# A graph network's convolution: adding and folding two tables of sums with strided reductions in the loop

## The chip, the cores and the metric

The kernel runs on one core of a Trainium2 chip. The metric is the device time of one execution in microseconds, and the median over several executions is compared. The engines of the core are PE (matrix products), DVE (vector work), ACT (activations and copies), POOL (here it only issues gathers from DRAM by index) and SP (here it only issues plain transfers).

## The reference

12500 nodes with 256 features, 212500 edges sorted by their target `dst`, and two layers. The first is a convolution, the second an attention; a residual and a layer norm follow each. What is computed around the change is the end of the first layer:

```python
mids = jnp.concatenate([mid0, mid1, mid2.reshape(-1, 3 * MUL), mid3.reshape(-1, 3 * MUL)], axis=1)
agg = jax.ops.segment_sum(mids, edge_dst, num_segments=n)
agg = agg * (1.0 / math.sqrt(NUM_NEIGHBORS))
z0a = agg[:, :MUL]
z0b = agg[:, MUL:2 * MUL]
z1a = agg[:, 2 * MUL:5 * MUL].reshape(n, MUL, 3)
z1b = agg[:, 5 * MUL:].reshape(n, MUL, 3)
o0 = (z0a @ lin2_w00 + z0b @ lin2_w01) * a * inv2
o1 = (jnp.einsum('nuc,uv->nvc', z1a, lin2_w10) + jnp.einsum('nuc,uv->nvc', z1b, lin2_w11)) * a[:, :, None] * inv2
```

`MUL` is 64, and `mid1` is itself a sum over three components; the kernel stores these three apart and adds them up per node, not per edge.

## The kernel before

**Stages.** `project_sources` writes a table of projected node rows (`y`). `convolve_in_order` (tensors named `sub_...`) is the first layer, `attend_in_order` (`ord_...`) the second. They run one after the other.

**The convolution's loop.** Edges come in tiles of 128. A group has 12 tiles (six pairs, numbered `u` from 0 to 5; four runs of three tiles), a turn of the loop three groups (`b` is 0, 1 or 2). There are 139 groups, so 47 turns. For each tile POOL issues one gather of 128 rows of `y` into `xg` (line 993). For each pair DVE multiplies these rows with edge weights (`products`, lines 1328 and 1333) and makes two selection matrices (line 1313); PE sums the products by target node into `psum_a` (`add_up`, line 1044) and makes the weights of a later pair (line 1024). ACT copies each run's sums out, and SP adds them to DRAM. It doesn't accumulate there: runs go in turn to one of two tables, `sums[0]` and `sums[1]`, each run over the zeros that the one before it in the same table had put behind its own rows. A node's sum is therefore the sum of its rows in both tables.

**Order.** Each engine walks the same list of steps, written by hand, and they meet in semaphores. POOL waits, ahead of every second tile, until PE has summed all but the last 8 to 10 tiles in front of it (`agg_done` at 12 g + k - 8 for tile k of group g). DVE waits for the rows, for the weights and for its buffers.

**The node step.** From the second turn on, each turn but the last also finishes one pair of node tiles (2 x 128 nodes): 45 pairs in the loop (`LOOP_PAIRS`), four in a tail behind it (`TAIL_PAIRS`). SP loads the pair's rows of both tables, those of `sums[0]` to `node_rows[:, 0]` and those of `sums[1]` to `loop_odds`, each 2 x 5 x 128 numbers wide (640 a node: chunk 0, three chunks for the three components, chunk 4). In the middle group, behind the products of pair 1, DVE runs `fold` for tile 0 and tile 1 of the pair (lines 1340 to 1353, called from `with_products`). It adds the two tables (line 1344, once for both tiles), waits for its own result, and then for each tile sums the left halves of chunks 1 to 3 into 64 numbers (line 1351) and copies their right halves beside them (line 1352), into `fold_rows`. PE turns chunk 0, the two halves of `fold_rows` and chunk 4 over (`turn_sums`, line 1057), tile 0 behind pair 2 and tile 1 behind pair 3 of the same group. Later in the turn come the products with `lin2`, the residual, the layer norm (statistics at line 1376, scaling at 1392, in the next turn) and the projection for the attention. `fold`, `turn_sums` and the rest are called for the four tail pairs too, whose second tables lie in `loop_odds` or in parts of `xg`.

Lines that the steps below name beside these: 2326 is the attention's gather on POOL, 2657 its leaky slope (`ord_raw` with itself), 2759 its weighting (`ord_xg` by `ord_prob`, which lies in PSUM), 266 a maximum in the set-up, 1364 and 1366 the residual's multiply-adds (the latter with every third number).

Of the kernel before, what the change touches and what calls it, by code (L numbers as in the profile page):

```python
# [22 lines left out]
AX = mybir.AxisListType.X  # L23

P = 128
# [3 lines left out]
MUL = 64  # L29
# [33 lines left out]
LOOP_PAIRS = SUB_TURNS - 2  # L63
TAIL_PAIRS = NODE_PAIRS - LOOP_PAIRS
# [40 lines left out]
def is_pair(i, n):  # L105

    return type(i) is int and i == n
# [646 lines left out]
def convolve_in_order(nc, io, c, y, sums, x1, xpa, att, kept):  # L754
# [10 lines left out]
    with Phase(nc, "sub", kept) as ph:  # L765
# [11 lines left out]
        agg_s = ph.sb("agg_s", [P, SUB_TURN, GROUP_SUBS, 4 * MUL])  # L777
        start_b = c["sub_start_b"]
        zeros = ph.sb("zeros", [P, SUM_WIDE])
        node_rows = ph.sb("node_rows", [P, TAIL_PAIRS, 2, 5, P])  # L780
        loop_odds = ph.sb("loop_odds", [P, 2, 5, P])
        spare = [xg[:, 1, 0:5], xg[:, 1, 5:10], xg[:, 2, 0:5]]
        node_odds = [loop_odds[:]] + [r.rearrange("p k f -> p (k f)").rearrange("p (j q f) -> p j q f", j=2, q=5)
                                      for r in spare]
        node_xt = ph.sb("node_xt", [P, TAIL_PAIRS, 2, 2, P])
        node_x = ph.sb("node_x", [P, TAIL_PAIRS, 2, FEAT])
        fold_rows = ph.sb("fold_rows", [P, 2, 2 * P])
        rows_t = ph.sb("rows_t", [P, 2, 4, P])
        pre = ph.sb("pre", [P, 2, FEAT])
        stats = ph.sb("stats", [P, 2, 6])  # L790
# [7 lines left out]
        psum_h = ph.ps("h", [P, 512])  # L798
        psum_w = ph.ps("w", [P, 4, 512])
# [14 lines left out]
        sums_in = [ph.sem(f"sums_in{n}") for n in range(TAIL_PAIRS)]  # L814
# [3 lines left out]
        both_added = ph.sem("both_added")  # L818
        folded, turned, turned_copied = ph.sem("folded"), ph.sem("turned"), ph.sem("turned_copied")
# [33 lines left out]
        def pair_rows(table, n):  # L853
# [4 lines left out]
        tail = [(LOOP_PAIRS + e, (e + 1) % TAIL_PAIRS, LOOP_PAIRS + 1 if e == TAIL_PAIRS - 1 else 1, (e + 1) % 2,  # L858
                 e // 2 + 1 + (LOOP_PAIRS if e % 2 else 0)) for e in range(TAIL_PAIRS)]

        with nc.Block(no_gpsimd_drain=True) as block:
# [141 lines left out]
            def _(pe):  # L1003
# [45 lines left out]
                    elif j == RUN - 1:  # L1049
                        mm.then_inc(evens_summed, 1)  # L1050

                def turn_sums(n, j, buf, bank):

                    pe.wait_ge(folded, 2 * n + j + 1)
                    for q, of in enumerate((node_rows[:, buf, j, 0], fold_rows[:, j, 0:P], fold_rows[:, j, P:],
                                            node_rows[:, buf, j, 4])):
                        mm = nc.tensor.transpose(bank[:, q * P:(q + 1) * P], of, c["ident"][:])
                    mm.then_inc(turned, 1)

# [31 lines left out]
                def bank_of_hidden(i, b, u, g):  # L1091

                    if normed_pair(i) and b == 0:
                        if u == 2:
                            if has(i, b, 1):
                                pe.wait_ge(silu_done, 2 * g + 4)
                            else:
                                pe.wait_ge(pre_done, LOOP_PAIRS)
                            turn_normed(i - 2, 0, psum_h)
                        if u == 3:  # L1100
                            project(i - 2, 0, psum_h)
                        if u == 4:
                            pe.wait_ge(p_copied, 2 * i - 3)
                            project(i - 2, 1, psum_h)
                    if sums_pair(i) and b == 1:
                        if u == 2:
                            pe.wait_ge(silu_done, 2 * g + 4)
                            turn_sums(i - 1, 0, 0, psum_h)
                        if u == 3:
                            pe.wait_ge(turned_copied, 2 * i - 1)  # L1110
                            turn_sums(i - 1, 1, 0, psum_h)
                    if sums_pair(i) and (b, u) == (2, 2):
                        pe.wait_ge(silu_done, 2 * g + 4)
                        add_self(i - 1, 0, i, psum_h)
# [42 lines left out]
                for e in range(TAIL_PAIRS + 1):  # L1157
                    if e == 0:
                        for j in range(2):
                            turn_sums(tail[0][0], j, tail[0][1], psum_w[:, j])  # L1160
                    if e < TAIL_PAIRS:
                        n, buf, times, _, _ = tail[e]
                        if e > 1:
                            pe.wait_ge(pre_done, n - 1)
                        add_self(n, buf, times, psum_w[:, 2 + e % 2])
                    if e > 0:
                        n, _, _, buf, _ = tail[e - 1]
                        if e > 1:
                            pe.wait_ge(t_copied, n)
                        turn_normed(n, buf, psum_a[0])  # L1170
                        for j in range(2):
                            pe.wait_ge(p_copied, 2 * n + j - 1)
                            project(n, j, (psum_a[1], psum_h)[j])
                    if e + 1 < TAIL_PAIRS:
                        n, buf, _, _, _ = tail[e + 1]
                        for j in range(2):
                            pe.wait_ge(turned_copied, 2 * n + j - 1)
                            turn_sums(n, j, buf, psum_w[:, j])

            @block.scalar  # L1180
            def _(act):
# [98 lines left out]
            def _(dve):  # L1280
# [39 lines left out]
                def products(g, b, i, u):  # L1320
# [16 lines left out]
                            .to_broadcast(shape), ALU.mult)  # L1337
                    a.then_inc(mids_done, 2)

                def fold(n, j, buf, times, first):  # L1340

                    if j == 0:
                        dve.wait_ge(sums_in[buf], 32 * times)
                        nc.vector.tensor_tensor(node_rows[:, buf], node_rows[:, buf], node_odds[buf],
                                                ALU.add).then_inc(both_added, 1)
                    if not first:
                        dve.wait_ge(turned, 2 * n + j - 1)
                    if j == 0:
                        dve.wait_ge(both_added, n + 1)
                    f, rows = fold_rows[:, j], node_rows[:, buf, j]  # L1350
                    nc.vector.tensor_reduce(f[:, 0:MUL], rows[:, 1:4, 0:MUL].rearrange("p q f -> p f q"), AX, ALU.add)
                    nc.vector.tensor_copy(f[:, MUL:].rearrange("p (q f) -> p q f", f=MUL), rows[:, 1:4, MUL:])\
                        .then_inc(folded, 1)
# [42 lines left out]
                def with_products(i, b, u):  # L1396

                    if normed_pair(i) and (b, u) == (0, 1):
                        normalise(i - 2, 0, None if is_pair(i, 2) else i - 2, is_pair(i, 2))
                    if sums_pair(i) and (b, u) == (1, 1):  # L1400
                        fold(i - 1, 0, 0, i, is_pair(i, 1))
                        fold(i - 1, 1, 0, i, is_pair(i, 1))
                    if sums_pair(i) and (b, u) == (2, 4):
                        add_x(i - 1, 0, i, psum_h, is_pair(i, 1))
                    if sums_pair(i) and (b, u) == (2, 5):
                        moments(i - 1)
# [1738 lines left out]
```

## Time and profile before

| | |
|---|---|
| time, median of 3 runs | 4435.05 us (4433.04 to 4443.15) |
| the profiled execution, its time | 4443.72 us |
| its span | 4442.3 us |
| granted TensorE clock, mean | 0.916 |
| PE, weight loads, DVE, ACT, POOL busy | 89%, 56%, 82%, 28%, 73% of the span |
| convolution's gathers (line 993) | 1662, the first at 83.4 us, the last at 2218.9 us |
| attention's gathers (line 2326) | 1666, from 2294.3 to 4397.7 us |

A row of the trace names the line, the engine, the operation, what it writes and from what, the shapes (partitions x numbers) and the count. In a time line the first two numbers are start and duration in microseconds, and a bracket at the end is the idle time of the engine before it, with what ended it. "issue" in such a bracket is idle time in which the engine waited for nothing that the profile shows. In a view of one line, three durations in nanoseconds stand as minimum/median/maximum, then the first and the last start. In a group of the page, the first number behind the bar is busy time in microseconds, the second the mean duration in nanoseconds, and behind the second bar stands the idle time ahead.

### The profile page before, as it was taken

What the parts mean: (1) busy time and instruction counts of PE and PEld (TensorE: products, weight loads), DVE (VectorE), ACT (ScalarE), POOL (GpSimd) and SP (SyncE); (2) the same over time, 40 slices, a digit from 0 to 9 for tenths busy, and PEclk for the clock granted to TensorE, in tenths of its full rate; (3) what the DMA queues carried; (4) which work ended last, traced back from release to release, by engine and by line L of the source; (5) the groups of instructions that cost most, each with busy time, mean ns of one, the idle gap of its engine ahead of it and who ended that gap; (6) DMA issues with size and microseconds to landing.
All of it is one profiled execution on the core that took longest, in us unless ns stands there. A gap on an engine that the chain in (4) does not pass through costs nothing. (4 is left out here: it accounts for less than half of the span.)

```text
span 4442.3 us, 107936 instructions
## 1 busy us (share of the span) xinstructions
PE 3946.7 (89%) x29492; PEld 2493.8 (56%) x29492; DVE 3633.5 (82%) x10373; ACT 1263.3 (28%) x3082; POOL 3245.2 (73%) x3375
## 2 busy tenths in 40 slices
PE   6899999999999999899958899889999888998997
PEld 5444444444444444444436666666667666666665
DVE  2788888888888888888838888888888888888887
ACT  4222222222222222222212222222232222222222
POOL 3777777777777777777727777777777777777774
PEclk8999999999999999999968888888888889888888
DMA  7666666666666667666644444444444444444443
GB/s 284 189 203 205 194 208 200 201 205 194 209 199 200 207 194 210 198 201 205 193 136 122 123 124 125 123 123 124 124 123 124 124 123 123 124 124 123 123 125 84
DMA packets 443567, 727.04 MB, mean 164 GB/s; under 512 B 147552, under 2 KB 279666, under 8 KB 443492
## 3 DMA queue, kind: packets, MB, share of 16 engines
q0 software_dynamic: 160832, 443.98, 36.6%
q1 hardware_dynamic: 282660, 282.22, 19.7%
q8 instruction: 28, 0.46, 0.0%
q14 instruction: 47, 0.39, 0.0%
HBM read 578.28 MB, written 147.55 MB: 163 GB/s over the span
## 5 line engine op out<-in xcount | busy, mean ns | idle before, releaser
L993 POOL DMA_INDIRECT sub_xg<-y_rows,sub_meta x1662 | 1627.5, 979 | 569.2 <-issue 447.4
L2326 POOL DMA_INDIRECT ord_xg<-xpa_rows,ord_meta x1666 | 1597.1, 959 | 510.9 <-issue 466.2
L2394 PE MATMUL ord_a<-ord_xg,ord_sel 128*128 128x264 f32 x3332 | 1126.9, 472 | 141.2 <-DVE ord_xg L2759 141.1
L1044 PE MATMUL sub_a<-sub_mids,sub_sel 128*32 128x128 f32 x13296 | 901.6, 308 | 183.1 <-DVE sub_mids L1333 181.3
L2394 PEld LDWEIGHTS ord_a<-ord_xg,ord_sel 128*128 128x128 f32 x3332 | 711.0, 235 | 282.1 <-DVE ord_xg L2759 157.6
L1333 DVE TENSOR_TENSOR sub_mids<-sub_w,sub_xg 128x384 f32<-128x384 f32 x1662 | 840.5, 547 | 0.0
L1044 PEld LDWEIGHTS sub_a<-sub_mids,sub_sel 128*32 128x32 f32 x13296 | 405.7, 110 | 602.2 <-DVE sub_mids L1333 308.2
L1328 DVE TENSOR_TENSOR sub_mids<-sub_w,sub_xg 128x256 f32<-128x256 f32 x831 | 349.5, 421 | 309.7 <-DMA sub_xg<-y_rows,sub_meta 247.0
L1024 PE MATMUL sub_w<-sub_fc,sub_ht 64*128 64x256 f32 x3324 | 592.2, 434 | 0.0
L2759 DVE TENSOR_TENSOR ord_xg<-ord_xg,ord_prob 128x1024 f32<-128x1024 f32 x476 | 510.3, 1072 | 0.2 <-issue 0.2
L1313 DVE SCALAR_TENSOR_TENSOR sub_sel<-sub_dve,sub_rel,sub_meta 128x128 f32<-128x128 f32 x1668 | 499.4, 341 | 0.0
L1024 PEld LDWEIGHTS sub_w<-sub_fc,sub_ht 64*128 64x128 f32 x3324 | 253.2, 187 | 348.0 <-issue 322.2
L2353 PEld LDWEIGHTS ord_i<-ord_ai,ord_sel_t 128*128 128x128 f32 x3332 | 424.4, 205 | 7.8
L2353 PE MATMUL ord_i<-ord_ai,ord_sel_t 128*128 128x8 f32 x3332 | 413.3, 264 | 0.0
L2460 ACT ACTIVATE ord_sel_t<-ord_s 128x512 f32<-128x512 f32 x476 | 257.0, 540 | 503.3 <-PE ord_s L2342 503.3
L1199 ACT ACTIVATE sub_agg_s<-sub_a 128x256 f32<-128x256 f32 x554 | 212.4, 383 | 604.0 <-PE sub_a L1044 551.1
L2342 PE MATMUL ord_s<-ident,ord_sel 128*128 128x128 f32 x1666 | 282.2, 288 | 57.8 <-ACT ord_sel_t L2460 57.4
L2342 PEld LDWEIGHTS ord_s<-ident,ord_sel 128*128 128x128 f32 x1666 | 192.5, 146 | 196.4 <-issue 182.9
L1011 PE MATMUL sub_h<-sub_es,sub_fc 128*128 128x384 f32 x556 | 266.5, 562 | 26.6 <-DMA sub_fc<-in_fc_w_dram 15.3
L1187 ACT ACTIVATE sub_ht<-sub_h 128x384 f32<-128x384 f32 x278 | 136.3, 490 | 469.4 <-PE sub_h L1011 463.1
L2583 DVE TENSOR_TENSOR ord_sel<-ord_rel,ord_dve 128x1792 f32<-128x1792 f32 x119 | 240.6, 2022 | 14.6
L2608 DVE TENSOR_TENSOR_SCAN ord_ahead<-ord_dve,ord_own 128x128 f32<-128x128 f32 x238 | 100.4, 422 | 93.2 <-ACT ord_own L2451 72.9
(199 smaller groups left out, 3749.2 us busy)
## 6 DMA issues: line engine op xcount, KB each, us to landing
sub_sum_rows<-sub_zeros SPq DMA_DIRECT2D x554, 80.0 KB
sub_sum_rows<-sub_agg_s SPq DMA_DIRECT2D x554, 64.0 KB
sub_node_rows<-sub_sum_rows SPq DMA_DIRECT2D x49, 640.0 KB, 5.8
sub_loop_odds<-sub_sum_rows SPq DMA_DIRECT2D x46, 640.0 KB
ord_xg<-xpa_rows,ord_meta POOLq DMA_INDIRECT x1666
sub_xg<-y_rows,sub_meta POOLq DMA_INDIRECT x1662
ord_x_rows<-x_rows SPq DMA_DIRECT2D x119, 128.0 KB, 2.1
out_dram<-ord_res SPq DMA_DIRECT2D x119, 128.0 KB
```

The lines of the kernel that those rows point to most:

```text
L993: nc.gpsimd.indirect_dma_start(xg[:, b, k], None, y, bass.IndirectOffsetOnAxis(ids[:, b, 0, k:k + 1], 0))\
L1011: nc.tensor.matmul(psum_h[:, 0:HALF_PAIRS * P], fc1[:], es[:, b, part], start=True, stop=True).then_inc(h_done, 1)
L1024: mm = nc.tensor.matmul(psum_w[:, 2 * (u % 2) + h, 0:4 * MUL], ht[part, b, u], fc2[part], start=True, stop=True, skip_group_check=True)
L1044: mm = nc.tensor.matmul(a[ROWS * m:ROWS * (m + 1), 0:w].rearrange("p (q f) -> p q f", f=MUL), sel[:, b, k, m], of, start=(j == 0), stop=(j ...
L1313: a = nc.vector.scalar_tensor_tensor(out=sel[:, b, k], in0=ramp.unsqueeze(1).to_broadcast(shape), scalar=rel[:, b, k:k + 1], in1=ea[:, b, ...
L1328: nc.vector.tensor_tensor(mids[:, d:d + 2, 0::7], w[:, :, 0:2], xg[:, b, 2 * u:2 * u + 2, 0:MUL].unsqueeze(2).to_broadcast([P, 2, 2, MUL]) ...
L1333: a = nc.vector.tensor_tensor(mids[:, d + h, 1:7].rearrange("p (q c) f -> p q c f", q=2), w[:, h, 2:4].unsqueeze(2).to_broadcast(shape), x ...
L2326: nc.gpsimd.indirect_dma_start(xg[:, b, k], None, xpa, bass.IndirectOffsetOnAxis(ids[:, b, k:k + 1], 0))\
L2342: last_mm = nc.tensor.transpose(psum_s[:, k % 4], sel[:, b, k], c["ident"][:])
L2353: last_mm = nc.tensor.matmul(psum_i[:, k * HEADS:(k + 1) * HEADS], sel_t[:, k], ai[:, b], start=True, stop=True, skip_group_check=True)
L2394: mm = nc.tensor.matmul(psum_a[b % 2][:, 0:WIDE], sel[:, b, k], xg[:, b, k], start=(k == 0), stop=(k == TILES - 1 and not has(i, b, -1)), ...
L2759: nc.vector.tensor_tensor(x, x, prob[:, k0:k1].unsqueeze(3).to_broadcast([P, k1 - k0, HEADS, HEAD_DIM]), ALU.mult).then_inc(msg_done, k1 - k0)
```

## The change

In the loop, the table of odd runs becomes a fifth entry of `node_rows`, a constant distance behind entry 0 (four entries, 20480 bytes a partition). A new `fold_in_loop` replaces `fold` there. It has no addition of the tables. For each tile it runs three reductions whose innermost axis is the pair of tables: one over tables and components together for the left halves (384 numbers to 64), one for the right halves (384 to 192), one for chunks 0 and 4 (512 to 256) into a new tensor `ends_rows`. `turn_sums` takes chunk 0 and chunk 4 from the place that it is given: `ends_rows` in the loop, `node_rows` in the tail. The tail keeps `fold`, and the count it waits for starts at the tail.

```diff
-        node_rows = ph.sb("node_rows", [P, TAIL_PAIRS, 2, 5, P])
-        loop_odds = ph.sb("loop_odds", [P, 2, 5, P])
+        node_rows = ph.sb("node_rows", [P, TAIL_PAIRS + 1, 2, 5, P])
+        loop_odds, loop_rows = node_rows[:, TAIL_PAIRS], node_rows[:, 0::TAIL_PAIRS]
...
+        ends_rows = ph.sb("ends_rows", [P, 2, 2, P])
...
-                def turn_sums(n, j, buf, bank):
+                def turn_sums(n, j, bank, first, last):
 
                     pe.wait_ge(folded, 2 * n + j + 1)
-                    for q, of in enumerate((node_rows[:, buf, j, 0], fold_rows[:, j, 0:P], fold_rows[:, j, P:],
-                                            node_rows[:, buf, j, 4])):
+                    for q, of in enumerate((first, fold_rows[:, j, 0:P], fold_rows[:, j, P:], last)):
...
-                            turn_sums(i - 1, 0, 0, psum_h)
+                            turn_sums(i - 1, 0, psum_h, ends_rows[:, 0, 0], ends_rows[:, 0, 1])
...
+                def fold_in_loop(n, j, times, first):
+
+                    if j == 0:
+                        dve.wait_ge(sums_in[0], 32 * times)
+                    if not first:
+                        dve.wait_ge(turned, 2 * n + j - 1)
+                    f, rows = fold_rows[:, j], loop_rows[:, :, j]
+                    nc.vector.tensor_reduce(f[:, 0:MUL], rows[:, :, 1:4, 0:MUL].rearrange("p d q f -> p f d q"),
+                                            mybir.AxisListType.XY, ALU.add)
+                    nc.vector.tensor_reduce(f[:, MUL:].rearrange("p (q f) -> p q f", f=MUL),
+                                            rows[:, :, 1:4, MUL:].rearrange("p d q f -> p q f d"), AX, ALU.add)
+                    nc.vector.tensor_reduce(ends_rows[:, j], rows[:, :, 0::4].rearrange("p d q f -> p q f d"),
+                                            AX, ALU.add).then_inc(folded, 1)
+
                 def fold(n, j, buf, times, first):
...
-                        dve.wait_ge(both_added, n + 1)
+                        dve.wait_ge(both_added, n - LOOP_PAIRS + 1)
...
                     if sums_pair(i) and (b, u) == (1, 1):
-                        fold(i - 1, 0, 0, i, is_pair(i, 1))
-                        fold(i - 1, 1, 0, i, is_pair(i, 1))
+                        fold_in_loop(i - 1, 0, i, is_pair(i, 1))
+                        fold_in_loop(i - 1, 1, i, is_pair(i, 1))
```

## Rows read from the trace of the kernel before

**Rows 1.** Page, part 1: busy us, share of the span, instructions, by engine.

```profile
PE 3946.7 (89%) x29492; PEld 2493.8 (56%) x29492; DVE 3633.5 (82%) x10373; ACT 1263.3 (28%) x3082; POOL 3245.2 (73%) x3375
```

**Rows 2.** Stretch: busy PE, PEld, DVE, ACT, POOL; clock, DMA, GB/s.

```profile
204.00:2148.00 1944.00, 1779.14 (x17459) 901.73 (x17457) 1633.18 (x4579) 545.20 (x1175) 1482.44 (x1514) 0.98 0.68 202
```

**Rows 3.** The gathers: page, part 5, then the view of line 993 (durations; idle).

```profile
L993 POOL DMA_INDIRECT sub_xg<-y_rows,sub_meta x1662 | 1627.5, 979 | 569.2 <-issue 447.4
...
L993 POOL DMA_INDIRECT sub_xg<-y_rows,sub_meta x1662: 951/957/2232, 83.4 to 2218.9; - x185
...
  issue: 447.4, 1467
```

**Rows 4.** DVE time line: addition in first turn, last turn, tail.

```profile
156.21 1.48 DVE L1344 TENSOR_TENSOR sub_node_rows<-sub_node_rows,sub_loop_odds 128x1280 f32<-128x1280 f32 x1
...
2192.36 1.48 DVE L1344 TENSOR_TENSOR sub_node_rows<-sub_node_rows,sub_loop_odds 128x1280 f32<-128x1280 f32 x1
...
2234.84 1.49 DVE L1344 TENSOR_TENSOR sub_node_rows<-sub_node_rows,sub_xg 128x1280 f32<-128x1280 f32 x1 [6.50 <-DMA sub_xg<-sub_sum_rows]
```

**Rows 5.** View of the waits, 200 to 2190 us: total, times, longest.

```profile
DVE sub_mids L1328 <- DMA sub_xg<-y_rows,sub_meta: 221.7, 251, 3.9
```

**Rows 6.** Time line of DVE, the turn near 1129 us: start, duration.

```profile
1128.97 1.48 DVE L1344 TENSOR_TENSOR sub_node_rows<-sub_node_rows,sub_loop_odds 128x1280 f32<-128x1280 f32 x1
...
1131.38 0.34 DVE L1352 COPY sub_fold_rows<-sub_node_rows 128x192 f32<-128x192 f32 x1
...
1131.64 0.41 DVE L1328 TENSOR_TENSOR sub_mids<-sub_w,sub_xg 128x256 f32<-128x256 f32 x1
```

**Rows 7.** Time line of POOL: gathers of three turns, in order of time.

```profile
156.59 1.93 POOL L993 DMA_INDIRECT sub_xg<-y_rows,sub_meta  x1 [0.30 <-issue]
...
1129.73 1.54 POOL L993 DMA_INDIRECT sub_xg<-y_rows,sub_meta  x1 [0.30 <-issue]
...
1131.58 0.96 POOL L993 DMA_INDIRECT sub_xg<-y_rows,sub_meta  x1 [0.30 <-issue]
...
1136.62 0.96 POOL L993 DMA_INDIRECT sub_xg<-y_rows,sub_meta  x1 [0.30 <-PE sub_a L1044]
...
2193.09 1.57 POOL L993 DMA_INDIRECT sub_xg<-y_rows,sub_meta  x1 [0.30 <-issue]
```

**Rows 8.** Time line of DVE and POOL at three other places, in pairs.

```profile
182.61 0.74 DVE L1376 BATCH_NORM_STATS2 sub_stats<-sub_pre 128x6 f32<-128x256 f32 x2
...
182.79 0.95 POOL L993 DMA_INDIRECT sub_xg<-y_rows,sub_meta  x1 [0.31 <-issue]
...
2328.16 1.21 DVE L2759 TENSOR_TENSOR ord_xg<-ord_xg,ord_prob 128x1024 f32<-128x1024 f32 x1
...
2328.32 0.97 POOL L2326 DMA_INDIRECT ord_xg<-xpa_rows,ord_meta  x1 [0.30 <-issue]
...
2361.03 0.39 DVE L2657 SCALAR_TENSOR_TENSOR ord_leaky<-ord_raw 128x224 f32<-128x224 f32 x1
...
2361.12 1.13 POOL L2326 DMA_INDIRECT ord_xg<-xpa_rows,ord_meta  x1 [0.30 <-issue]
```

**Rows 9.** Groups of DVE by line and form: busy us, mean ns, idle before.

```profile
L1344 DVE TENSOR_TENSOR sub_node_rows<-sub_node_rows,sub_loop_odds 128x1280 f32<-128x1280 f32 x46 | 68.0, 1479 | 0.0
...
L1366 DVE SCALAR_TENSOR_TENSOR sub_pre<-sub_h,pair_factor,sub_node_x 128x192 f32<-128x192 f32 x90 | 42.3, 470 | 0.0
...
L1351 DVE TENSOR_REDUCE sub_fold_rows<-sub_node_rows 128x64 f32<-128x192 f32 x98 | 36.0, 368 | 5.4 <-DVE sub_node_rows L1344 0.5
...
L1352 DVE COPY sub_fold_rows<-sub_node_rows 128x192 f32<-128x192 f32 x98 | 33.7, 343 | 0.0
...
L1364 DVE SCALAR_TENSOR_TENSOR sub_pre<-sub_h,pair_factor,sub_node_x 128x64 f32<-128x64 f32 x90 | 24.9, 277 | 3.7 <-issue 3.7
...
L266 DVE TENSOR_REDUCE spans<-sub_reach 1x1 f32<-1x556 f32 x1 | 0.7, 709 | 0.0
```

**Rows 10.** Time line of PE, the sums behind the fold.

```profile
1133.04 1.07 PE L1044 MATMUL sub_a<-sub_mids,sub_sel 128*32 128x128 f32 x16 [1.11 <-DVE sub_mids L1333]
```

More of the change, by code:

```diff
@@ L779, in convolve_in_order @@
         zeros = ph.sb("zeros", [P, SUM_WIDE])
-        node_rows = ph.sb("node_rows", [P, TAIL_PAIRS, 2, 5, P])
-        loop_odds = ph.sb("loop_odds", [P, 2, 5, P])
+        node_rows = ph.sb("node_rows", [P, TAIL_PAIRS + 1, 2, 5, P])
+        loop_odds, loop_rows = node_rows[:, TAIL_PAIRS], node_rows[:, 0::TAIL_PAIRS]
         spare = [xg[:, 1, 0:5], xg[:, 1, 5:10], xg[:, 2, 0:5]]
-        node_odds = [loop_odds[:]] + [r.rearrange("p k f -> p (k f)").rearrange("p (j q f) -> p j q f", j=2, q=5)
+        node_odds = [loop_odds] + [r.rearrange("p k f -> p (k f)").rearrange("p (j q f) -> p j q f", j=2, q=5)
                                       for r in spare]
@@ L1107, in bank_of_hidden @@
                             pe.wait_ge(silu_done, 2 * g + 4)
-                            turn_sums(i - 1, 0, 0, psum_h)
+                            turn_sums(i - 1, 0, psum_h, ends_rows[:, 0, 0], ends_rows[:, 0, 1])
                         if u == 3:
                             pe.wait_ge(turned_copied, 2 * i - 1)
-                            turn_sums(i - 1, 1, 0, psum_h)
+                            turn_sums(i - 1, 1, psum_h, ends_rows[:, 1, 0], ends_rows[:, 1, 1])
                     if sums_pair(i) and (b, u) == (2, 2):
@@ L1159, in _ @@
                         for j in range(2):
-                            turn_sums(tail[0][0], j, tail[0][1], psum_w[:, j])
+                            turn_sums(tail[0][0], j, psum_w[:, j], node_rows[:, tail[0][1], j, 0],
+                                      node_rows[:, tail[0][1], j, 4])
                     if e < TAIL_PAIRS:
@@ L1177, in _ @@
                             pe.wait_ge(turned_copied, 2 * n + j - 1)
-                            turn_sums(n, j, buf, psum_w[:, j])
+                            turn_sums(n, j, psum_w[:, j], node_rows[:, buf, j, 0], node_rows[:, buf, j, 4])
             @block.scalar
```

## The prediction

> **What bounds the kernel now.** I read the views in this order: busy shares, two stretches, one line of POOL, then single instructions in one turn of the loop.
>
> By the busy shares PE leads (89%) and POOL comes third with 73% [rows 1], which misleads. In the convolution's loop POOL is busy 1482.44 us of 1944, PE 1779.14 [rows 2]. But POOL's idle time is almost all "issue" (447.4 us in 1467 pieces, about 0.30 us each): the engine's own pause between two gathers, in which it waits for nobody [rows 3]. So its true load is a gather (median 957 ns) plus a pause of 447.4/1467 = 0.305 us, together 1.262 us. A turn of the loop has three groups of 12 tiles, so 36 gathers, 45.4 us. A turn takes (2192.36 - 156.21)/44 = 46.28 us, measured from the fold's big addition in the first turn that has one to that in the last [rows 4]. POOL alone fills the turn up to 0.85 us. DVE, on the other hand, waits for rows to land: 221.7 us in 251 waits between 200 and 2190 us (43 turns), some 5 us a turn [rows 5]. PE and DVE have room; the gather queue sets the pace. The chain of waits doesn't help here: its pieces begin only in the attention, behind the convolution, so the time line of POOL must do.
>
> Where are the missing 0.8 us? Look at the turn near 1129 us. DVE's addition of the two tables runs from 1128.97 to 1130.45 [rows 6]. POOL's gather that starts inside it, at 1129.73, takes 1.54 us where others take 0.96 [rows 7]. It ends at 1131.27, 2.30 us after the addition began. In the first turn the addition starts at 156.21 and the gather begun at 156.59 takes 1.93 us: its end is 158.52, 2.31 after. In the last the gather begun at 2193.09 takes 1.57 us and ends at 2194.66, 2.30 after 2192.36 [rows 4, 7]. I laid all 1662 gathers beside DVE's instructions: in each of the 45 turns with an addition exactly one gather starts in it, each is stretched (1.38 to 2.23 us) and ends about 2.3 us after the addition's start, wherever it began. Only three others of the 1662 are over 1.0 us, the longest of them 1.08. So the gather is held at its start until the addition has read its inputs (2.30 - 0.96 = 1.35 us after its start), then runs its normal 0.96 us. The sum: 1662 gathers at a mean of 979 ns and a median of 957 ns [rows 3] give 1627.5 - 1662 x 0.957 = 37.0 us in all, or 0.82 us in each of 45 turns, which closes the gap of the turn.
>
> **Which DVE instructions hold POOL.** The addition reads two tensors in SBUF. Three contrasts [rows 8]: statistics, with one SBUF input, had started at 182.61 when a gather began at 182.79 (0.95 us, unstretched, as all 38 such gathers); a 1.21 us multiplication of the attention, whose second input lies in PSUM (ord_prob), had begun at 2328.16 before a gather at 2328.32 (0.97 us; none of 333 is stretched); the leaky slope reads ord_raw twice from SBUF, and the gather begun 0.09 us after it takes 1.13 us (23 of 43 are over 1 us). So two SBUF inputs hold it and one doesn't, whatever the length. One rule states the contrary for this very case: the Trainium skill, "SBUF — State Buffer", section "Who interferes with whom", infers that `tensor_tensor`, taking only the shared read interface, doesn't stall descriptor generation; by that the addition's removal would give 0 and the time would stay at 4435 us. The 45 stretched gathers speak against it. The same section says a `tensor_reduce` never contends on trn2, with which the contrasts agree.
>
> **The change, part by part.**
>
> 1. The addition goes from the loop (45 x 1.48 us of DVE). The four of the tail stay, the first of them at 2234.84 [rows 4]; the last gather of the convolution starts at 2218.9, so none runs beside them [rows 3]. With it the hold of POOL goes: -37.0 us on the queue that sets the pace. Nothing takes its place if reductions with one input behave like the statistics.
>
> 2. DVE's fold becomes longer. Before, from the addition's start to the next product: 1131.64 - 1128.97 = 2.67 us [rows 6], for one addition (1479 ns), two reductions of 192 elements (368 ns) and two copies of 192 (343 ns) [rows 9]. After: per tile two reductions of 384 elements and one of 512. No row shows reductions of this size or with their two halves 20 KB apart. The slope from the copy of 192 to the addition of 1280 is (1479 - 343)/1088 = 1.04 ns an element; from the reduction of 192 to the one of 556 it is (709 - 368)/364 = 0.94. With 1.04, taken because that pair has the full width of 128 partitions: 368 + 200 = 568 twice and 368 + 333 = 701, sum 1.84 us. An instruction starts about 0.08 us before the end of the one in front (the copy at 1131.38 takes 0.34, the product behind it starts at 1131.64 [rows 6]), so 1.60 us a tile and 3.19 a turn: +0.52 us. With 0.94 it is +0.38. The other end: the reductions run at half rate, 2.08 ns an element. Then 168 + 384 x 2.08 = 967 twice and 1233, 2.93 us a tile, 5.85 a turn: +3.2 us.
>
> 3. What covers this. Queued behind the fold on DVE are the products, on which PE waited already: 1.11 us before its sums at 1133.04, which end at 1134.11 [rows 10]. They will start 0.52 us later. POOL is only stopped when a gather's tile is more than the allowed lead ahead of PE's sums; the gather that needs these sums is the one at 1136.62 [rows 7], 2.51 us after them. The change takes from both sides: POOL comes 0.82 us earlier, PE 0.52 us later. 1.17 us are left, so the longer fold costs nothing, and DVE's 5 us of waits a turn take it up before the next one. What is late next is still the gather.
>
> 4. Edits with one answer. PE's four transposes a tile read another buffer of the same shape; tile 0 is folded 1.7 us after the start and tile 1 at 3.3, still before the sums that PE runs ahead of them end (1134.11, 5.1 us after it [rows 10]): 0. The wait of DVE on its own addition goes (under 0.1 us, DVE only). One DVE instruction more in each turn counts above. SP's loads, their number and order stay: 0. The tail does what it did: 0.
>
> Sum: -37.0 us. The profiled execution took 4443.7 us (span 4442.3), the median of the runs shown is 4435.05, 8.7 less; I take the same difference from it: 4406.7 profiled, **4398.0 us** as median. The rest of the kernel, attention, runs by the same kind of queue and isn't touched.
>
> **Rivals.**
>
> A. The long reductions hold POOL too. About 3.19/1.26 = 2.5 gathers start in the fold; each would wait for the rest of an instruction of 0.6 us, 0.3 on average, 0.76 us a turn. Net -0.06 x 45 = -3 us: 4432. Against it: the unstretched gathers over one-input instructions. For it: no row has a gather starting in a reduction of any length worth the name.
>
> B. Reads that hop at every element cost more than 1.04 ns. For it: the multiply-add with stride-3 operands (192 elements, 470 ns) against its plain one of 64 (277 ns) gives 1.51 ns an element [rows 9], 0.47 too much. Against it: the present reduction of 192 hops at every element (three chunks, 512 bytes apart) and costs only 25 ns more than a copy of 192. With 0.47 on 2560 elements the fold grows by 0.52 + 1.20 = 1.72 us, and 2.51 - 0.82 - 1.72 = -0.03: just covered. Above that each microsecond counts; up to a growth of 2.51 us the gain shrinks to nothing, so 4398 to 4435, middle 4416. The Trainium skill, "Vector Engine (DVE) Microarchitecture Reference", section 5.2 "Measured stream behaviour on trn2", gives about 0.65 cycle an element for such hops, but full rate for one source alternating between two regions 16 KiB apart; with its dearer figure (0.68 ns) the same sum gives +2.25 us, a net of 0.26 us a turn, 4423, as an estimate.
>
> C. Slower: the same price at half rate, in the reductions of the fold. Growth 3.18 us; the lead lacks 3.18 + 0.82 - 2.51 = 1.49 us, POOL waits that long in each turn, and the turn grows by 1.49 - 0.82 = 0.67 us: 45 x 0.67 = +30, **4465 us**. It decides from a fold (both tiles) longer than 2.67 + 2.51 = 5.2 us.
>
> D. A later link. The gathers come faster, but a later link (landing of rows, PE near 91% in the loop) takes half of it: 4416. PE has 46.28 x (1 - 1779/1944) = 3.9 us a turn free [rows 2], more than 0.82.
>
> E. The hold doesn't come from the addition's two inputs, but from something that the fold keeps, its first instruction behind the wait for the tables. Then the gather that starts in the fold is held 0.8 us as before and the gain is 0: 4435. The Trainium skill's inference above would lead here. Against it: the gather's end follows the addition's start by 2.30 us in every turn, and the gather at 1131.58, begun in the second copy (1131.38), takes 0.96 us [rows 6, 7], as do those of all 45 turns.
>
> **How the numbers follow.** Forecast 77%, A 7%, B 5%, C 4%, D 4%, E 3%. A measurement of this kernel tells about 0.2% (9 us) from no change. Faster by more than that: the forecast, D and half of B, 0.84. Within it: E, the other half of B and most of A, 0.10. Slower: C, and the part of A in which the held gathers cost more than the average taken, 0.06. Range: the forecast with its spread of runs (some 6 us) and the milder ends of B and D, 4391 to 4424; A, C and E are left out, 14%.
>
> **What would show it.** Right: no gather over 1.1 us in the convolution apart from the first, L993's mean 957 to 960 ns and its sum near 1591 us; turns of 45.45 us; reductions of some 570, 570 and 700 ns; DVE's big addition only 4 times, in the tail; DVE busy some 35 us more in all; POOL's gaps still 0.30 us. A is seen in gathers over 1 us that end a fixed time after a reduction. B and C in reductions over 750 ns and in gaps of POOL over 0.4 us, released by PE's sums, six to ten gathers after the fold. D in such gaps elsewhere. The prediction is wrong if the stretch of the gathers isn't caused by the two SBUF inputs but by something of the fold that remains.

## The result, and the profile after

The changed kernel takes 4470.14 us (median; 4468.32 to 4476.36) against 4436.51 us before (4433.04 to 4443.15): a ratio of 1.0067, 95% interval 1.0055 to 1.0079. It is slower by 0.7%, clear of the noise. The forecast was 4398 us, its range 4391 to 4424.

The page of the kernel after: busy times, and the group of the gathers (mean 959 ns; before 979 [rows 1, 3]).

```profile
PE 3970.3 (89%) x29492; PEld 2509.4 (56%) x29492; DVE 3673.0 (82%) x10418; ACT 1263.5 (28%) x3082; POOL 3217.2 (72%) x3375
...
L994 POOL DMA_INDIRECT sub_xg<-y_rows,sub_meta x1662 | 1594.0, 959 | 630.6 <-issue 418.9
```

The view of that line. Durations are minimum/median/maximum in ns, then come the idle times ahead of it.

```profile
L994 POOL DMA_INDIRECT sub_xg<-y_rows,sub_meta x1662: 952/960/1087, 85.1 to 2246.5; - x185
...
  issue: 418.9, 1356
...
  PE sub_a L1045: 149.5, 305
```

No gather is held any more: the longest takes 1087 ns, where it was 2232 [rows 3]. 33.5 us of POOL's busy time are gone. But "PE sub_a" stands at 149.5 us in 305 pieces, which is 0.49 each and so more than the pause of 0.305. Taken piece by piece, 81 gaps of the loop are longer than 0.4 us, and they exceed the ordinary pause by 58 us. POOL gave back more than it gained. The convolution's gathers run from 85.11 to 2246.54 us, 2161.4, against 2135.5 before: +25.9 us of the +32.6 in the span. 1.7 us lie ahead of the first gather and 5.0 behind the last.

The view of the waits in 42 turns of the loop after (total us, times, longest):

```profile
PE sub_a L1045 <- DVE sub_mids L1334: 161.7, 88, 2.4
...
DVE sub_mids L1329 <- PE sub_w L1025: 155.4, 292, 3.0
...
POOL sub_xg L994 <- PE sub_a L1045: 134.3, 278, 1.8
...
DVE sub_mids L1329 <- DMA sub_xg<-y_rows,sub_meta: 53.2, 49, 2.6
```

DVE waited 221.7 us for rows before [rows 5] and now 53.2; it waits for PE's weights instead (155.4 us, against 41.2 in as long a stretch before). PE waits for DVE's products in fewer and longer pieces: 161.7 us in 88, against 154.2 in 139 before. The three reductions, in groups by form (busy us, mean ns):

```profile
L1348 DVE TENSOR_REDUCE sub_fold_rows<-sub_node_rows 128x64 f32<-128x384 f32 x90 | 72.5, 806 | 0.0
...
L1352 DVE TENSOR_REDUCE sub_ends_rows<-sub_node_rows 128x256 f32<-128x512 f32 x90 | 61.3, 681 | 0.0
...
L1350 DVE TENSOR_REDUCE sub_fold_rows<-sub_node_rows 128x192 f32<-128x384 f32 x90 | 49.3, 548 | 0.0
```

548 and 681 ns are near the 568 and 701 of the forecast. The sum over two axes takes 806.

Now one turn. In DVE's time line after, the fold begins at 1049.11, and the next product starts at 1052.70, 3.59 us later (2.67 before [rows 6]).

```profile
1049.11 0.82 DVE L1348 TENSOR_REDUCE sub_fold_rows<-sub_node_rows 128x64 f32<-128x384 f32 x1
...
1052.70 0.41 DVE L1329 TENSOR_TENSOR sub_mids<-sub_w,sub_xg 128x256 f32<-128x256 f32 x1
```

PE's time line of the same turn: sums, weights, sums, weights.

```profile
1054.09 1.07 PE L1045 MATMUL sub_a<-sub_mids,sub_sel 128*32 128x128 f32 x16 [2.12 <-DVE sub_mids L1334]
...
1055.09 1.04 PE L1025 MATMUL sub_w<-sub_fc,sub_ht 64*128 64x256 f32 x4
...
1057.11 1.84 PE L1045 MATMUL sub_a<-sub_mids,sub_sel 128*32 128x128 f32 x16
...
1058.88 0.70 PE L1025 MATMUL sub_w<-sub_fc,sub_ht 64*128 64x256 f32 x4
```

PE was idle for 2.12 us. Behind that, four products for the weights take 1.04 us and sixteen for the sums 1.84 us. In another turn, 47 us later, the same groups take 0.70 and 1.07 us, behind an idle time of 2.02:

```profile
1101.35 1.07 PE L1045 MATMUL sub_a<-sub_mids,sub_sel 128*32 128x128 f32 x16 [2.02 <-DVE sub_mids L1334]
...
1102.35 0.70 PE L1025 MATMUL sub_w<-sub_fc,sub_ht 64*128 64x256 f32 x4
...
1103.57 1.07 PE L1045 MATMUL sub_a<-sub_mids,sub_sel 128*32 128x128 f32 x16
```

The view by stretches shows why. Its columns are PE, PEld, DVE, ACT and POOL busy, granted clock, DMA share and GB/s; the rows are 42 turns, then 5 us of the slow turn and 5 us of the quick one.

```profile
205.36:2172.44 1967.08, 1793.36 (x17474) 913.00 (x17473) 1670.75 (x4622) 546.36 (x1176) 1450.87 (x1513) 0.97 0.67 199
1054.00:1059.00 5.00, 4.91 (x42) 2.41 (x44) 4.20 (x13) 0.98 (x2) 2.88 (x3) 0.66 0.60 162
1101.00:1106.00 5.00, 4.65 (x55) 2.62 (x59) 5.00 (x15) 1.09 (x3) 3.27 (x5) 1.00 0.56 163
```

In the slow turn the granted clock averages 0.66 of full speed over these 5 us: for a part of it PE ran at 1.2 GHz instead of 2.4. In the quick turn it is 1.00. The average of the loop, 0.97 against 0.98 before [rows 2], hides it. The Trainium skill, "TensorE: Matmul & The Clock Gate", part 1, knows the two levels and that idle time lowers the clock; the trace agrees on both. POOL's time line shows what follows; three gathers of the slow turn, the last row the quick turn's.

```profile
1054.03 0.96 POOL L994 DMA_INDIRECT sub_xg<-y_rows,sub_meta  x1 [0.30 <-issue]
...
1055.91 0.96 POOL L994 DMA_INDIRECT sub_xg<-y_rows,sub_meta  x1 [0.92 <-PE sub_a L1045]
...
1059.71 0.95 POOL L994 DMA_INDIRECT sub_xg<-y_rows,sub_meta  x1 [1.57 <-PE sub_a L1045]
...
1103.17 0.96 POOL L994 DMA_INDIRECT sub_xg<-y_rows,sub_meta  x1 [0.82 <-PE sub_a L1045]
```

The gather at 1055.91 starts 0.75 us after PE's sums end (1055.16). The next gated one comes 1.57 us behind the gather in front of it, because the sums from 1057.11 ended at 1058.95 instead of 1058.2. The quick turn has the first of these waits (0.82) and not the second.

### The profile page after: what moved, and what is told of

Same layout as the page of the kernel before. It is cut to its first block and busy times, and to the rows that moved or that the text cites. A ratio compares the mean times of both kernels' runs of the same rounds, so it can differ in the third digit from the quotient of the medians.

```text
span 4474.9 us, 107936 instructions
## 1 busy us (share of the span) xinstructions
PE 3970.3 (89%) x29492; PEld 2509.4 (56%) x29492; DVE 3673.0 (82%) x10418; ACT 1263.5 (28%) x3082; POOL 3217.2 (72%) x3375
## 5 line engine op out<-in xcount | busy, mean ns | idle before, releaser
L994 POOL DMA_INDIRECT sub_xg<-y_rows,sub_meta x1662 | 1594.0, 959 | 630.6 <-issue 418.9
L1045 PE MATMUL sub_a<-sub_mids,sub_sel 128*32 128x128 f32 x13296 | 914.8, 311 | 184.7 <-DVE sub_mids L1334 184.5
```

The costliest lines, as they stand in the source:

```text
L994: nc.gpsimd.indirect_dma_start(xg[:, b, k], None, y, bass.IndirectOffsetOnAxis(ids[:, b, 0, k:k + 1], 0))\
L1045: mm = nc.tensor.matmul(a[ROWS * m:ROWS * (m + 1), 0:w].rearrange("p (q f) -> p q f", f=MUL), sel[:, b, k, m], of, start=(j == 0), stop=(j ...
```

## The experiments

The change lengthened the fold, and PE is idle there for longer. Two explanations of the loss are tried: that PE's clock falls behind the longer idle time (the clock theory), and that DVE's products, and with them PE's sums, simply come later (the lateness theory). The kernel before was run again beside each set of kernels (4436.5 to 4443.9 us; in brackets in the table), so a kernel is judged by its ratio to that. A turn is measured from fold to fold, in one profiled execution of each kernel; a fall of the clock is told by PE's groups of sums over 1.2 us or of weights over 0.8 us. PE has two idle times in each turn that matter here: that of the fold, and that of the statistics, behind the residual and the statistics at the end of a turn, ahead of the next turn's first sums. The table stands ahead of the runs, since each of them is read by it.

| kernel | time, us (before beside it) | turn, us | PE idle at the fold, us | turns whose clock fell there | and at the statistics |
|---|---|---|---|---|---|
| before | 4436.5 | 46.28 | 1.2 | 0 | 18 of 44 |
| after | 4470.1 (4436.5) | 46.84 | 2.0 | 27 of 43 | 3 |
| e1 | 4453.1 (4443.9) | 46.5 | filled | 1 of 44 | 23 |
| e2 | 4427.5 (4443.9) | 45.9 | 1.3 | 0 | 19 of 44 |
| e3 | 4467.9 (4443.9) | 46.8 | 2.0 | 29 of 43 | 1 |
| e4 | 4468.4 (4443.9) | 46.8 | 2.0 | 27 of 43 | 3 |
| e5 | 4412.9 (4442.7) | 45.45 | 1.3 | 0 | filled, 0 |
| e6 | 4426.2 (4442.7) | 45.83 | filled | 0 | filled, 0 |
| e7 | 4440.5 (4442.7) | 46.1 | 1.2 | 0 | filled, 0 |
| e8 | 4440.3 (4442.7) | 46.2 | 0.7 | 0 | 20 of 44 |
| e9 | 4472.5 (4441.3) | 46.9 | 2.0 | 29 of 43 | 2 |
| e10 | 4475.6 (4441.3) | 47.0 | 2.0 | 33 of 43 | filled, 0 |
| e11 | 4441.8 (4441.3) | 46.2 | 1.3 | 0 | filled, 0 |
| e12 | 4411.1 (4441.3) | 45.47 | 1.3 | 0 | filled, 0 |

**e1.** After, with products on PE in the fold's idle time.

```diff
@@ bank_of_hidden, sums_pair(i) and b == 1 @@
+                        if u == 1:
+                            for _ in range(4):
+                                nc.tensor.matmul(psum_a[1][:, FEAT:2 * FEAT], c["w_proj"][:, 0, 0:P],
+                                                 c["w_proj"][:, 0, 0:FEAT], start=True, stop=True,
+                                                 skip_group_check=True)
```

> The changed kernel, with four extra products on PE (128 by 256, about 1.1 us, their result unused) behind the sums of pair 1 in the middle group, where PE waits for DVE's fold. Clock theory: the longer fold leaves PE idle for 2.0 to 2.1 us, and behind that the granted clock is at the lower level for some 3 us in about 30 of 44 turns, worth 1.5 us each. With the filler PE is idle about 1.0 us, the clock stays at the upper level, turns take 45.5 to 45.8 us, all of them: 4400 to 4420 us. Lateness theory: DVE's products come 0.9 us later and the gathers wait for PE's sums because of that alone; the filler changes nothing in it: 4465 to 4480 us, and turns of 47.2 us remain.

Measured: 4453.1 us, ratio 1.0019 (1.0009 to 1.0028). The node sums that this kernel gets are others than the reference's; the steps and sizes are the same. The extra products start anew (`start=True`) in a bank in which sums are in progress; those of e5 and e6, in the same columns of such a bank but without a new start, leave the sums right. The time lies between both theories, and the table says why: the clock no longer falls at the fold (1 turn), but now at the statistics (23 turns), where it had fallen in only 3. Turns with a fall take 47.08 us on average, those without 45.82. The clock's price is confirmed; its place was wrong.

**e2.** After, with the fold of tile 1 a pair later.

```diff
                     if sums_pair(i) and (b, u) == (1, 1):
                         fold_in_loop(i - 1, 0, i, is_pair(i, 1))
+                    if sums_pair(i) and (b, u) == (1, 2):
                         fold_in_loop(i - 1, 1, i, is_pair(i, 1))
```

> The changed kernel, with the fold of tile 0 behind the products of pair 1 as before and that of tile 1 behind those of pair 2. PE then waits twice for about 1.8 us less its lead instead of once for 3.6. Clock theory and lateness theory both: no gather waits for PE, no lower clock, turns of 45.45 us: 4395 to 4405 us. If the hold of the gathers by the addition was not worth 37 us after all (say because rows landed no sooner), 4430 to 4440 us.

Measured: 4427.5 us, ratio 0.9962 (0.9949 to 0.9974): faster than before, but less than expected. PE's time line shows the idle time of the statistics (1.78 us) and the longer of the two that the fold now causes (1.27 us, in place of one of 2.0).

```profile
1060.10 1.07 PE L1045 MATMUL sub_a<-sub_mids,sub_sel 128*32 128x128 f32 x16 [1.78 <-DVE sub_mids L1334]
...
1084.80 1.07 PE L1045 MATMUL sub_a<-sub_mids,sub_sel 128*32 128x128 f32 x16 [1.27 <-DVE sub_mids L1334]
```

No turn has a fall at the fold; 19 have one at the statistics, and they take 46.65 us against 45.32 of the others. I had not reckoned with the second place.

**e3.** After, with the gathers allowed two tiles more.

```diff
-    LEAD = 10
+    LEAD = 12
```

> The changed kernel with one number changed: the gathers may run 12 tiles ahead of PE's sums instead of 10. If the wait of the gathers for PE is the only way in which PE's lateness reaches the end, turns take 45.5 to 45.7 us even where the clock falls: 4400 to 4412 us. If PE at the lower clock is itself the limit: 4450 to 4475 us.

Measured: 4467.9 us, ratio 1.0054 (1.0037 to 1.0071), turns of 46.8 us as in the kernel after. The waits of 42 turns (total us, times, longest):

```profile
DVE sub_mids L1329 <- PE sub_w L1025: 210.9, 375, 1.5
...
POOL sub_xg L994 <- PE sub_a L1045: 125.3, 254, 1.6
```

The wait for rows is down to 1.0 us (it was 53.2), that for PE's weights has risen from 155.4 to 210.9, and the gathers wait for PE about as long as before. So POOL's wait was not the bottleneck but a consequence. PE and DVE hand their work back and forth, and this pair takes 46.8 us a turn however far ahead the rows lie.

**e4.** The kernel before, its fold made as long as after's.

```diff
                         fold(i - 1, 0, 0, i, is_pair(i, 1))
+                        nc.vector.tensor_reduce(extra[:], node_rows[:, 0, :, 0:3], AX, ALU.add)
                         fold(i - 1, 1, 0, i, is_pair(i, 1))
```

> The kernel before, with its addition, and one more reduction of 768 elements between the two tiles' folds (its result unused): the fold takes about 3.5 us, as long as in the changed kernel, and the addition still holds one gather a turn. Clock theory: PE idles 2 us, the clock falls in many turns: 4455 to 4500 us. Lateness theory: 0.9 us of the 2.5 us of spare are used, nothing else happens: 4432 to 4442 us.

Measured: 4468.4 us, ratio 1.0057 (1.0040 to 1.0074): the change's loss without the change. PE idles 1.97 us, and the clock falls there in 27 of 43 turns, as in this row, where the sums take 1.43 us instead of 1.07:

```profile
1147.34 1.43 PE L1045 MATMUL sub_a<-sub_mids,sub_sel 128*32 128x128 f32 x16 [1.97 <-DVE sub_mids L1334]
```

Only the length of the fold (3.53 us) differs from the kernel before, whose 45 held gathers it keeps. What the lengthened fold costs is thus shown, and with it that the hold costs next to nothing once PE and DVE set the pace: with it e4 loses about as much as the kernel after does without it (1.0057 against 1.0067, the intervals overlap); that the clock carries most of it is left to e6.

**e5.** e2 with products on PE ahead of a turn's first sums.

```diff
@@ add_up @@
+                    if (b, k) == (0, 0) and (type(i) is not int or i > 1):
+                        for _ in range(4):
+                            nc.tensor.matmul(a[:, FEAT:2 * FEAT], c["w_proj"][:, 0, 0:P],
+                                             c["w_proj"][:, 0, 0:FEAT], start=False, stop=False,
+                                             skip_group_check=True)
                     if k == 0:
                         pe.wait_ge(sel_done, g + 1)
```

> The kernel of e2 (changed, fold in two places) with four products on PE (about 1.1 us, their result unused, into spare columns) ahead of a turn's first sums, where PE idles 1.78 us behind the residual and the statistics on DVE. In e2 the clock fell behind that idle time in 19 of 45 turns. Clock theory: no idle time of PE over 1.6 us is left, the clock falls hardly ever, the gathers alone set the pace: turns of 45.5 us, 4400 to 4410 us. Theory that the two engines' hand-over itself (not the clock) is the limit in e2: as e2, 4425 to 4435 us.

Measured: 4412.9 us, ratio 0.9934 (0.9917 to 0.9951). Stretch of 42 turns, columns as above:

```profile
205.92:2115.15 1909.23, 1828.26 (x17809) 953.66 (x17808) 1669.08 (x4622) 545.70 (x1176) 1447.04 (x1513) 1.00 0.69 206
```

The clock is 1.00, a turn takes 45.46 us, which is 36 gathers at 1.262. It is the pace that the forecast had for the change; the time lies just above the expected 4400 to 4410. DVE waits for rows again, and PE's waits for DVE are short:

```profile
DVE sub_mids L1334 <- DMA sub_xg<-y_rows,sub_meta: 106.6, 113, 2.5
...
PE sub_a L1050 <- DVE sub_mids L1339: 66.5, 91, 1.4
```

This kernel is faster than both the kernel before and the kernel after.

**e6.** After with its fold in one place, such products at both places (the edit is shown against e5's condition).

```diff
-                    if (b, k) == (0, 0) and (type(i) is not int or i > 1):
+                    if ((b, k) == (0, 0) and (type(i) is not int or i > 1)) or ((b, k) == (1, 4) and sums_pair(i)):
```

> The changed kernel with its fold as it is, and such products on PE at both places: ahead of the sums of pair 2 in the middle group (the fold's 2.0 us of idle time) and ahead of a turn's first sums. Clock theory: nearly no turn with the lower clock, turns of 45.5 us: 4400 to 4412 us. Lateness theory (the longer fold costs by its length): 4440 us or more, with gathers that wait for PE's sums in most turns.

Measured: 4426.2 us, ratio 0.9967 (0.9954 to 0.9979), outside both expectations, between them.

```profile
204.98:2129.72 1924.74, 1897.60 (x18145) 1017.54 (x18144) 1667.89 (x4621) 545.62 (x1176) 1446.86 (x1513) 1.00 0.69 204
```

The fold is as long as after's, and the clock never falls. A turn takes 45.83 us. Hence the parts: 46.84 - 45.83 = 1.01 us a turn are the clock's, and 45.83 - 45.45 = 0.38 us are the lateness itself (in 37 of 44 turns gathers in the 12 us behind the fold's start wait for PE beyond their pause, over all turns 0.36 us a turn). Both theories held a part, the clock nearly three quarters.

**e7.** The kernel before with e5's products.

> The kernel before with the products ahead of a turn's first sums only. It has a lower clock behind that idle time in 19 of 45 turns. If it is bound by its gathers (36 of them at 1.262 us and one held for 0.82 us), the lower clock is covered and its removal gives nothing: 4433 to 4444 us, turns of 46.28 us. If its turns are bound by PE and DVE, it gets some 0.4 to 0.7 us a turn faster: 4410 to 4425 us.

Measured: 4440.5 us, ratio 0.9994 (0.9984 to 1.0004): no difference. The kernel before had 18 turns with a lower clock at the statistics and lost nothing by them that can be measured: its gathers set the pace. The profiled execution has turns of 46.1 us instead of the 46.28 expected; its held gathers take 29.5 us too much instead of 37.0, which is the same 0.17 us a turn. Two such idle times of the kernel before, 1.78 us each, and the weights behind them:

```profile
648.68 1.07 PE L1044 MATMUL sub_a<-sub_mids,sub_sel 128*32 128x128 f32 x16 [1.78 <-DVE sub_mids L1333]
...
649.68 0.70 PE L1024 MATMUL sub_w<-sub_fc,sub_ht 64*128 64x256 f32 x4
...
879.85 1.59 PE L1044 MATMUL sub_a<-sub_mids,sub_sel 128*32 128x128 f32 x16 [1.78 <-DVE sub_mids L1333]
...
881.36 1.23 PE L1024 MATMUL sub_w<-sub_fc,sub_ht 64*128 64x256 f32 x4
```

After the first the clock stays up (1.07, 0.70), after the second it is down (1.59, 1.23).

**e8.** The kernel before with the fold in two places, as e2.

> The kernel before, with its addition, and the fold of tile 1 moved behind the products of pair 2. If the gathers' pace and the addition's hold of one gather bind it, nothing is gained: 4433 to 4444 us, one gather of 1.4 to 2.3 us in each turn. If the gain of e2 came from the two places alone, 4420 to 4430 us.

Measured: 4440.3 us, ratio 0.9994 (0.9985 to 1.0004). The gathers:

```profile
L993 POOL DMA_INDIRECT sub_xg<-y_rows,sub_meta x1662: 952/957/2270, 85.9 to 2218.9; - x185
```

They are held as ever (45 of them). PE's idle time at the statistics is 1.8 to 1.9 us here. e2's gain therefore needs the addition's removal, and the two places alone give nothing.

**e9.** After, the first reduction reading in another order.

```diff
-rows[:, :, 1:4, 0:MUL].rearrange("p d q f -> p f d q")
+rows[:, :, 1:4, 0:MUL].rearrange("p d q f -> p f q d")
```

> The changed kernel, the first reduction of each tile reading its six numbers in another order: for each component the two tables, instead of for each table the three components. It took 0.81 us for 384 numbers where the second reduction, also of 384, takes 0.55. If the price lies in the order of reading, it takes 0.55 to 0.58 us, the fold 3.1 us instead of 3.6, PE idles about 1.55 us there, which was not followed by the lower clock in e2 and e5, and only the idle time behind the statistics is: 4422 to 4438 us. If a sum over two axes is slow in itself, it stays at 0.81 us and the time at 4465 to 4475 us.

Measured: 4472.5 us, ratio 1.0069 (1.0052 to 1.0086), as after.

```profile
L1348 DVE TENSOR_REDUCE sub_fold_rows<-sub_node_rows 128x64 f32<-128x384 f32 x90 | 72.5, 806 | 0.0
```

806 ns: the order isn't the price. What makes the sum over two axes some 260 ns longer than the one over a single axis (548 ns, also 384 numbers read) stays open. The 1.55 us of idle time that the expectation took as tried in e2 and e5 didn't stand there at the fold: it was 1.3 us.

**e10.** e9 with e5's products.

> The kernel of e9 with the products on PE ahead of a turn's first sums (as in e5), the fold in one place. By the clock theory and the size of the fold: lower clock in no turn, PE's lateness 0.5 us less than in e6, so no gather waits: turns of 45.45 to 45.6 us, 4408 to 4418 us. If e5's gain needs the fold in two places, 4425 to 4432 us.

Measured: 4475.6 us, ratio 1.0080 (1.0063 to 1.0097), outside both expectations. The forecast rested on a shorter fold, which e9 didn't give. What it shows is that the second filler alone is useless while PE idles 2.0 us at the fold: the clock falls there in 33 of 43 turns.

**e11 and e12.** e5 with one more DVE instruction of 1280 numbers a turn, once with two inputs in SBUF, once with one.

```diff
+                    if sums_pair(i) and (b, u) == (2, 1):
+                        twice = zeros[:].unsqueeze(1).to_broadcast([P, 2, SUM_WIDE])
+                        nc.vector.tensor_tensor(extra[:], twice, twice, ALU.add)
...
+                        nc.vector.tensor_reduce(extra[:, 0, 0:2], twice, AX, ALU.add)
```

> The kernel of e5 with one more addition of 1280 numbers with two inputs in SBUF on DVE in each turn, behind the products of pair 1 of the last group (the result is unused), 1.48 us. If two inputs in SBUF hold a gather that starts meanwhile: one gather of 1.4 to 2.3 us in each turn, turns of about 46.3 us, some 35 us more than e5. If the hold came from something else in the old fold: gathers of 0.96 us, the same time as e12.

> The kernel of e5 with one more reduction of 1280 numbers (one input in SBUF) at the place of e11's addition, 1.5 us, its result unused. If one input doesn't hold gathers: no gather over 1.1 us; the time of e5 or, if DVE's 1.5 us more are no longer covered there, up to 15 us more. If any long DVE instruction holds a gather, as e11.

Measured: e11 4441.8 us, ratio 1.0003 (0.9993 to 1.0012); e12 4411.1 us, ratio 0.9937 (0.9920 to 0.9953). The added instruction and the gathers, e11:

```profile
L1427 DVE TENSOR_TENSOR sub_extra<-sub_zeros 128x1280 f32<-128x1280 f32 x45 | 66.5, 1478 | 0.0
...
L995 POOL DMA_INDIRECT sub_xg<-y_rows,sub_meta x1662: 951/957/2267, 86.8 to 2220.3; - x185
```

and e12:

```profile
L1427 DVE TENSOR_REDUCE sub_extra<-sub_zeros 128x2 f32<-128x1280 f32 x45 | 66.3, 1472 | 0.0
...
L995 POOL DMA_INDIRECT sub_xg<-y_rows,sub_meta x1662: 951/957/1090, 86.8 to 2187.3; - x185
```

1478 and 1472 ns at the same place: the longest gather is 2267 ns in the one and 1090 in the other, and the times are 30.7 us apart. In e11 the held gathers together take 36 us too much, nearly as much as the old addition's (37). Two things differ between the two, the second input and the size of the result (1280 numbers against 2). The attention of the kernel before tells these apart. Its `ord_sel` has one input in SBUF (`ord_rel`), the other in PSUM (`ord_dve`), and writes 1792 numbers to SBUF:

```profile
2341.93 2.02 DVE L2583 TENSOR_TENSOR ord_sel<-ord_rel,ord_dve 128x1792 f32<-128x1792 f32 x1
...
2342.21 0.95 POOL L2326 DMA_INDIRECT ord_xg<-xpa_rows,ord_meta  x1 [0.30 <-issue]
```

175 gathers start while it runs, and the longest takes 0.97 us. A long result in SBUF doesn't hold them; the second input in SBUF is left. The four kernels with such an addition (before, e7, e8, e11) have turns within 0.1 us of 45.45 plus their held time.

## Why the prediction was wrong, point by point

**The bound, and part 1, the hold.** Right. The addition held one gather in each turn, it is the second SBUF input that does it (e11 against e12, with `ord_sel` against the size of the result), and its removal is worth the predicted 37 us where nothing else binds: e5's gathers run from 87.2 to 2186.35 us, 2099.2 against 2135.5, 36.4 less. Counted by the gathers that start while the instruction runs, the prediction's three contrasts hold 46, 350 and 37 gathers, not 38, 333 and 43; none, none and 23 of them are stretched, so the reading stands. Rivals A and E are out. The Trainium skill, "SBUF — State Buffer", section "Who interferes with whom", infers that such an addition leaves descriptor generation alone, and e11 speaks against it. The prediction took this for the section's whole word; the same section also says that a DVE instruction with two SBUF inputs contends with a GpSimd instruction that reads SBUF. The trace agrees with that: the gather's rows name `sub_meta`, which lies in SBUF, as an input. The section's sentence that a reduction never contends agrees with e12 (1.09 us at most).

**Part 2, the length.** The direction and the form were right, the size wasn't. Three reductions a tile take 2.04 us, not 1.84, the fold 3.59 us, not 3.19: +0.92 instead of +0.52. All of it is the sum over two axes, 806 ns instead of 568; the other two came out 20 ns under their forecast. I had no row of it and took it at the price of a sum over one. Rival B's price (a hop at every element) gives 748, 748 and 942 ns for the three, which took 806, 548 and 681: it is not the price of a hop. Rival C named almost the measured time, 4465 us, by a mechanism that didn't occur: it needed a fold over 5.2 us.

**Part 3, the cover.** This step failed, in three ways. First, the spare of 2.51 us was taken from the end of PE's sums to the start of the gather, as if a release took no time; the kernel after shows 0.75 us between these when the gather really waits. 2.51 - 0.75 - 0.82 - 0.92 = 0.02 us: nothing left. Even that is too much: in the two turns shown, slow and quick, the gather behind the fold waits 0.62 and 0.52 us beyond its pause. Second, "PE has 3.9 us a turn free" and "DVE waits 5 us a turn" are sums over a turn. The idle time of PE lies where DVE has a long piece of its own to do, and no other part of the turn made up for it; e3 shows that with rows in plenty the pair of PE and DVE still needs the same time. Together this is the lateness, 0.38 us a turn. Third, and largest, I named PE as the engine that waits 1.11 us in the fold and made that 1.6 without asking what idle time does to PE. The granted clock fell behind the 2.0 us in 27 of 43 turns, and in 3 others at the statistics; a turn with a fall takes 47.26 us at the fold, one without any 45.80. (27 x 1.46 + 3 x 1.28)/43 = 1.01 us a turn, as much as e6 gives back. The loop's mean of 0.98 [rows 2] had already contained falls in 18 turns, hidden behind the gathers; a mean over turns couldn't show them, a look at single turns would have.

**The sum again.** -0.82 for the hold, +0.38 for lateness, +1.01 for the clock: +0.57 us a turn, 45 turns, +26 us. The gathers' stretch grew by 25.9. The terms are differences between the turns of before, e5, e6 and after, so they must add up; what supports them apart from that is the count of falls, which gives 1.01 by itself. The span grew by 32.6: the first gather starts 1.7 us later, and what follows the last takes 5.0 us more. In the other kernels this remainder varies from 2219.7 to 2227.1 us, against 2223.4 before and 2228.4 after, so part of these 5 us may belong to the single execution; that wasn't settled.

**Parts that held.** The transposes from the new tensor, SP's transfers and the tail cost nothing that can be seen. D, a later link that takes part of the gain, comes closest to what happened, with the wrong size: I gave it half of the 0.82 us a turn, and it took 1.39.

## What to carry to other kernels

When one queue sets the pace by less than 2%, removing its delay only exposes the next bound, so work that bound out with the same care, turn by turn and with release times included. Ask of each idle time of TensorE that an edit lengthens what the granted clock does behind it, in the turns one by one and not in a mean. And where gathers issued by GpSimd set the pace, look at the long DVE instructions with two inputs in SBUF beside them; a version with one input can be worth having though it is no shorter: here it gave 0.68 us for each of 45 instructions of 1.5 us (e12 against e11).

## What the runs showed of the hardware that I had not expected

- A gather issued by GpSimd that starts while DVE runs an addition with both inputs in SBUF waits at its start (0.96 us became up to 2.27 us in e11); beside a reduction of the same length it doesn't (1.09 us at most in e12). The 37 gathers of the kernel before that were already running when the addition began took 0.96 us at most.
- TensorE's granted clock fell behind the idle time at the statistics (1.8 us, 1.8 to 1.9 in e8) in 18 of 44 turns before, 23 in e1, 19 in e2, 20 in e8, and behind 2.0 us in 27 to 33 of 43. Behind 1.2 to 1.3 us, in the turns of e2, e5, e7, e11 and e12, it never did. The same idle time is followed by a fall in one turn and by none in the next. And in the 43 turns of the kernel after, a fall at the fold (27) was never followed by another at the statistics; the 3 falls there are in turns that have none at the fold. Why one turn and not another was not tried.
- Some 1.1 us of products whose results nobody uses, in an idle time of 1.78 us, removed these falls and were worth some 13.5 us (e5 lies 29.9 us under the kernel before beside it, e2 16.4). In the kernel before they are worth nothing (e7).
- A sum over two axes of 384 numbers into 64 took 806 ns, whichever axis is read first (after and e9); one over a single axis of 384 into 192 took 548.
